# Low parts of two key tiles in one GpSimd instruction, and value products one step later

## The reference

```python
# x: 1 x 2048 x 512; 32 heads in 8 groups, 64 wide
h = layernorm(x)
y = rmsnorm(h) * rms_w
q, k, v = split(y @ w_in.T)          # q has 4 heads per group, k and v one
q, k = rope(q), rope(k)
attn = softmax(causal(q @ k.T / 8))  # per head, 2048 x 2048
x = x + h + (attn @ v) @ w_out.T
z = layernorm(x)
out = x + (silu(z @ wu.T) * (z @ wg.T)) @ wd.T   # ternary weights wu, wg, wd
```

## Time and profile before

| | us |
|---|---|
| median of 3 runs | 2073.79 (2073.11 to 2074.5) |
| span of the profiled execution, first to last instruction | 2071.1 |
| PE busy, whole span | 1946.6 (94%) |
| PE weight loads | 1183.4 (57%) |
| DVE busy | 1202.1 (58%) |
| ACT busy | 934.7 (45%) |
| POOL busy | 1499.9 (72%) |
| low parts on POOL (L788), 1280 instructions | 1136.6 |

### The profile page before, as it was taken

How to read it: one execution, slowest core, us unless ns; L and a number is a source line. 1 busy time by engine, 2 the same in 40 slices (tenths; PEclk the granted TensorE clock), 3 DMA queues, 4 the chain that set the end, 5 groups by cost and what they waited for, 6 DMA issues and landing times. The chain is left out here.

```text
span 2071.1 us, 55258 instructions
## 1 busy us (share of the span) xinstructions
PE 1946.6 (94%) x21382; PEld 1183.4 (57%) x21382; DVE 1202.1 (58%) x3156; ACT 934.7 (45%) x1969; POOL 1499.9 (72%) x1755
## 2 busy tenths in 40 slices
PE   4799989999999999999999999999969998999998
PEld 3466656666666666666666666666634444444443
DVE  7577558757765874776677477657714652221221
ACT  4355645555655555555555555555641211111110
POOL 2599989999999999999999999999950001221221
PEclk8899999999999999999999999999989999999999
DMA  6232262223224222322432242332236630000000
GB/s 202 60 62 40 53 165 52 46 54 69 45 51 85 60 45 50 73 43 53 85 61 45 48 76 43 53 67 64 38 122 214 227 108 1 16 5 20 5 16 21
DMA packets 301573, 136.79 MB, mean 66 GB/s; under 512 B 248336, under 2 KB 285456, under 8 KB 299792
## 3 DMA queue, kind: packets, MB, share of 16 engines
q1 hardware_dynamic: 301328, 133.43, 27.7%
HBM read 49.48 MB, written 25.17 MB: 36 GB/s over the span
## 5 line engine op out<-in xcount | busy, mean ns | idle before, releaser
L788 POOL TENSOR_TENSOR pl<-p 128x512 f16<-128x512 f32 (+3 forms) x1280 | 1136.6, 916 | 62.9 <-ACT p L647 62.2
L647 ACT ACTIVATE p<-a_ps 128x512 f32<-128x512 f32 (+3 forms) x1280 | 671.6, 532 | 633.7 <-PE a_ps L580 390.1
L714 DVE TENSOR_REDUCE mpart<-a_ps 128x1 f32<-128x512 f32 x768 | 518.0, 687 | 145.3 <-PE a_ps L564 139.2
L596 PE MATMUL a_ps<-v,p 128*128 128x65 f16 x4352 | 528.6, 193 | 30.4 <-POOL pl L788 25.6
L598 PE MATMUL a_ps<-v,p 128*128 128x64 f16 x4352 | 531.1, 194 | 0.0
L600 PE MATMUL a_ps<-v,pl 128*128 128x65 f16 x4352 | 528.1, 192 | 0.0
L596 PEld LDWEIGHTS a_ps<-v,p 128*128 128x128 bf16 x4352 | 412.5, 97 | 150.3 <-ACT p L647 39.2
L564 PE MATMUL a_ps<-k_hl,q_hh 128*128 128x512 f16 (+3 forms) x1280 | 441.7, 350 | 33.4 <-DMA q_hh<-qk_hi 8.6
L598 PEld LDWEIGHTS a_ps<-v,p 128*128 128x128 bf16 x4352 | 406.3, 98 | 99.6 <-issue 0.2
L580 PE MATMUL a_ps<-q_lm,k_h 128*128 128x512 f16 (+3 forms) x1280 | 445.7, 348 | 0.0
L579 PE MATMUL a_ps<-q_hh,k_hl 128*128 128x512 f16 (+3 forms) x1280 | 444.9, 348 | 0.0
(11 more groups left out here) (96 smaller groups left out, 2308.4 us busy)
## 6 DMA issues: line engine op xcount, KB each, us to landing
attn_scratch<-o_turn SPq DMA_DIRECT2D x64, 256.0 KB, 3.0
p_att<-attn_scratch SPq DMA_DIRECT2D x32, 512.0 KB, 4.3
raw<-ffn_t SPq DMA_DIRECT2D x12, 1024.0 KB, 5.0
wraw<-w_in_t SPq DMA_DIRECT2D x8, 768.0 KB, 5.5
resid_scratch<-raw SPq DMA_DIRECT2D x4, 1024.0 KB, 4.3
raw<-w_out_t SPq DMA_DIRECT2D x1, 4096.0 KB, 16.8
x<-resid_scratch SPq DMA_DIRECT2D x4, 1024.0 KB, 8.2
out<-x SPq DMA_DIRECT2D x16, 256.0 KB, 2.1
```

The source lines that it names most:

```text
L596: nc.tensor.matmul(o, weights, v[:, par, j, 0:VU], start=(j == 0 and t == 0), stop=False, skip_group_check=True)
L647: nc.scalar.activation(p32[:, i % RING, r * P:CHUNK], sbank(i)[:, r * P:CHUNK], ACT.Exp, scale=SCALE).then_inc(exp_done, 1)
L714: nc.vector.reduce_max(mpart[:, u % 2, t, kk:kk + 1], bank, AX.X).then_inc(maxs_used, 1)
L788: nc.gpsimd.tensor_tensor(pl[:, i % RING, cols], p32[:, i % RING, cols], p_high[:, i % RING, cols], ALU.subtract).then_inc(low_ready, 1)
```

## The change

`low_part` makes nothing at an even full step; at the odd one behind it, it makes the low parts of both, in one instruction over two neighbouring ring slots (1024 columns), and raises `low_ready` by two. It waits for the later of the two exponentials. Diagonal steps keep one instruction each. A unit's full steps begin at an even step and come in multiples of four, and the ring has ten slots, so a pair never wraps. `PV_LAG` goes from 5 to 6: values i are issued after scores i + 6, a group ends with six value steps without scores, and `HIGH_LAG`, `LOW_OUT_LAG`, the place of `unit_out` and the due steps of `turn` and `store` move by one step with it.

```diff
--- before.py
+++ after.py
@@ -202,7 +202,7 @@
 FIRST_STEP = [sum(KEY_TILES[:u]) for u in range(UNITS + 1)]
 STEPS = FIRST_STEP[UNITS]
 PIECES = STEPS
-PV_LAG = 5
+PV_LAG = 6
 RING = 10
 SBANKS = 3
 SIDE = 3
@@ -230,6 +230,15 @@
 def score_bank(i):
 
     return i % SBANKS if i < STEPS - 1 else 1
+
+
+def low_span(i):
+
+    u, j = step_of(i)
+    full = TPC * (u // HG)
+    if j < full:
+        return (i - 1, i) if j % 2 else None
+    return (i, i)
 
 
 def bank_before(i):
@@ -781,12 +790,14 @@
             pool.wait_ge(ones_set, 2)
             def group(g, par, part):
                 def low_part(i, ahead=0):
+                    if not (span := low_span(i)):
+                        return
                     u, j = step_of(i)
                     r = first_query_tile(u // HG, j)
-                    cols = slice(r * P, CHUNK)
+                    part_of = lambda a: a[:, span[0] % RING:span[0] % RING + i - span[0] + 1, r * P:CHUNK]
                     pool.wait_ge(exp_done, (g + ahead) * STEPS + i + 1 + EXP_AHEAD)
-                    nc.gpsimd.tensor_tensor(pl[:, i % RING, cols], p32[:, i % RING, cols], p_high[:, i % RING, cols],
-                                            ALU.subtract).then_inc(low_ready, 1)
+                    nc.gpsimd.tensor_tensor(part_of(pl), part_of(p32), part_of(p_high),
+                                            ALU.subtract).then_inc(low_ready, i - span[0] + 1)
 
                 def rope_sum(ahead, t):
                     b = t % TILES_KEPT
```

## The result

The changed kernel takes 2094.73 us (median of 4 runs, 2093.75 to 2096.27), the kernel before beside it 2073.56: a ratio of 1.0103, 95% interval 1.0089 to 1.0117. It is slower by 21.2 us; forecast were 7.8, and the range ended at 2094. Lines have moved: pieces are L573, scores L588, values L605, exponentials L656, low parts L799, `weights_low` L713 (L704 before), `reduce_piece` L723.

A forecast was written before the change was run, and what follows sets the result against it. PE's own work was taken to bound the kernel, POOL only in two short places. Terms +10.2 - 1.6 - 2.4 + 1.6 = +7.8 us, added to the median 2073.8, gave 2081.5 us; range 2067 to 2094.

The forecast's parts named there:

- What bounds the kernel: PE's own work sets the time over most of a group; POOL sets it only near steps 26 to 31 and 152 to 159.
- Rival (1): POOL is the bound as its share suggests, so pairing pays and its waits go: 2052 us, chance 0.14.
- (2): The values' later place covers the stall near steps 26 to 31 and only the ends gain: 2071.4 us, chance 0.17.
- first place: Near steps 26 to 31: stall grows from 1.5 to 2.8 us per group, +10.2 us over eight groups.
- The pair: One POOL instruction of 1024 columns costs 1.85 us by starts, saving 0.144 us per pair, 55 us of POOL's time.
- Rival (3): A pair costs what two instructions cost, 2.00 us: about +20, 2094 us, chance 0.11.
- Step (c): Values run one step later, so a deadline moves by 0.64 us and scores come 0.36 us earlier.
- Second place: At a group's end, steps 152 to 159: -0.23 us per group, -1.6 us over seven groups.
- last group: No work ahead for a next group, POOL runs there without a gap: pairs gain 2.4 us.
- waits for DVE: PE waits 0.27 us longer at step 54, eight times, and 0.09 less at step 89, seven times: +1.6 us.
- Edits at nothing: Elsewhere the pair's delay stays below the slack, costing nothing; with that cover gone, up to 0.85 us per group each place.
- Its own sign of being wrong: The prediction is wrong if pairs wait elsewhere too: new PE waits for `pl` between 672 and 795 us.

The follow-up runs named there:

- pairs_lag5: The kernel before with the pairs but without the sixth step, values still five steps behind: 2097.20 us, ratio 1.0114.
- lag_only: The kernel before with only `PV_LAG` raised from 5 to 6, every low part keeping its own instruction: 2099.84 us, ratio 1.0124.
- single_in_units4_5: The changed kernel with low parts made one by one in units 4 and 5 (steps 16 to 31): 2083.49 us, ratio 1.0044.
- single_in_units4_5_9: The changed kernel with low parts made one by one in units 4, 5 and 9: 2073.52 us, ratio 1.000.
- lag_no_two_input_dve: The kernel before with values six steps behind and `weights_low` on DVE replaced by a one-operand reduction: 2071.36 us, ratio 0.9992.
- pairs_only_unit9: The kernel before (lag 5) with pairs in unit 9 alone, 32 in all: 2087.23 us, ratio 1.0061.
- pairs_no_two_input_dve: The changed kernel with `weights_low` on DVE replaced by a one-operand reduction: 2079.81 us, ratio 1.0029.

## Why the prediction was wrong

- **What bounds the kernel**: right. POOL's share was no bound; its work fell by 52 us and the time rose. Rival (1) is out, and so is (2): the first place didn't stay covered.
- **The pair**: right, 1.89 us as shown. Rival (3) needed 2.05 as shown and is out, although its 2094 us is near the result: its time would have come from other places. The estimate of 2.2 us, worked out from the Trainium skill's 2.6 cycles (GPSIMD Engine Reference, "Performance versus the Vector engine"), is too long for this form.
- **First place**: right in place, cause and size (+11.0 for +10.2): POOL idle ahead of pair 16/17, then waits at scores 24, values 24 and values 26. Step (c), within it, was too large: pairs_lag5 shows 0.11 us per group, and with low parts one by one the first place has 11.6 to 12.9 us with six steps (lag_only, single_in_units4_5, single_in_units4_5_9 and lag_no_two_input_dve), against 12.2 with five. So the size owes something to luck: the same working without (c) gives 3.4 us per group for the pairs with five steps, and pairs_lag5 has 3.0; at six steps two errors cancel, 2.8 against 2.9.
- **Second place, last group, waits for DVE**: right to some 0.2 us each.
- **Edits at nothing**: this step failed: "Elsewhere the pair's delay stays below the slack that the earlier trace rows show as no wait". I asked who waits for POOL's result, found slack, and stopped. A longer POOL instruction also holds up an instruction on DVE that waits for no semaphore of POOL's at all, so no row of waits named POOL. The earlier trace rows do have PE waiting 0.4 us for `mpart` at step 69: there DVE had no slack left to lose. It costs 15.1 us, 2.2 per group, where the prediction held a lost cover to be worth at most 0.85. Its own sign of being wrong, new waits for `pl` in this stretch, didn't come: the new waits are for `mpart`. pairs_only_unit9 shows the loss for the pairs alone (12.7 us of stall), and pairs_no_two_input_dve that the two-operand form carries it. The sixth step, costed at nothing too, costs 26 us through the same instruction when it is alone.
- **The evidence was in the trace of before**: the same shape took 612 ns in `normalise` and 950 in attention. I read POOL's shapes and not DVE's. The Trainium skill (SBUF — State Buffer, "SBUF: two separate sides") says that a DVE operation with two SBUF inputs and a GpSimd operation that reads SBUF exclude each other for a whole instruction, and that the one that starts first goes first. The runs here agree with that in 98 of 104 meetings by themselves (0.61 us becomes up to 1.42 beside 512 columns and 2.24 beside 1024). In the other six DVE's shown start lies 0.05 us or less ahead of a GpSimd instruction's, and DVE waited for that one too, up to 1.49 and 2.35 us. The 6.3 us of lag_only are more than that rule says.

## What to carry to other kernels

Before making one engine's instruction longer, look for an instruction of one shape whose mean duration differs between stages of the same trace: it may be held up by something that no row of waits names, as here, and then a longer neighbour makes it worse. An engine without a visible wait has slack only for its consumers, not for those that share a resource with it. Then merge instructions only where the merged engine itself sets the pace for several merges in a row, so that what they save outweighs a later first half: 2065 us here (with `weights_low` moved), against 2095 for merging everywhere.

## What the runs showed of the hardware

- A DVE instruction with two SBUF operands (128x384, 0.61 us) and GpSimd's two-operand instruction exclude each other: 1.39 us beside 512 columns back to back, 2.24 beside 1024. It lasts what is left of the GpSimd instruction plus 0.42 us. A DVE reduction with one SBUF operand keeps its 0.55 us, one from PSUM its 0.68, and `masked`, with one operand from each, its 0.67 to 0.69.
- The GpSimd instruction behind such a DVE instruction is 0.31 us longer (1.35 for 1.04, 2.20 for 1.89).
- In one kernel (lag_only) the DVE instruction missed five boundaries in a row in five of 28 cases (5.0 to 6.33 us), each time until GpSimd's row of instructions was over. In 104 meetings in programs made for it, four missed one boundary and none missed two.
- At each of these five cases PE waited 3.8 to 5.1 us, and near the end of the wait the granted clock fell to 1.2 of 2.4 GHz for 3.4 or 6.8 us.
